# Hybrid block on one core: another order of the units of a head pair in the attention stage

## The reference, cut to what matters

```python
x = x + conv(gn(x))          # 8 images x 64 channels x 32x32; 9 bilinear samples of 4 corners each
t = to_tokens(x)             # 8 x 1024 tokens x 64
# attention: 16 heads of 64, causal, rotary, on layer-normed tokens
q, k, v = proj(ln_t(t));  q, k = rope(q), rope(k)
att = softmax(where(causal, q @ k.T / 8, -inf));  t = t + (att @ v) @ w_o.T
t = t + spectral(ln_t(t))
# inside conv: out = einsum('bkhwc,ock->bohw', sampled, w), where sampled is the
# weighted sum of 4 gathered corners for each of 9 taps
```

## Time and profile before

| | |
|---|---|
| median of 3 runs | 2944.49 us (2943.2 to 2948.28) |
| the profiled execution | 2945.84 us |
| its span | 2944.1 us |
| TensorE busy, mean granted clock | 2745.4 us (93%), 0.965 |
| VectorE, ScalarE, GpSimd busy | 2185.9, 1329.4, 1736.8 us |

### The profile page before, as it was taken

One profiled execution on the slowest core, in us unless ns is written; L12 is line 12 of the kernel. 1 busy time (PEld: TensorE's weight loads), 2 busy tenths in 40 slices (PEclk: granted clock), 3 DMA queues, 4 the chain that ended last, 5 costly groups with the idle time before them and its releaser, 6 DMA issues. The chain is left out here.

```text
span 2944.1 us, 60697 instructions
## 1 busy us (share of the span) xinstructions
PE 2745.4 (93%) x18761; PEld 1792.2 (61%) x18761; DVE 2185.9 (74%) x3909; ACT 1329.4 (45%) x1788; POOL 1736.8 (59%) x1832
## 2 busy tenths in 40 slices
PE   3638999999999999999999999999998799999998
PEld 1324565565655655655655655655655688888887
DVE  3446878888778788778788888888876675767676
ACT  1103444444444444444444444444443465656565
POOL 3745777777777777777777777777776670000000
PEclk8658999999999999999999999999999899999999
DMA  5541221222222222222222222243443553434343
GB/s 151 145 110 53 59 64 54 72 63 63 64 62 62 65 61 62 63 63 62 63 63 62 64 59 65 64 61 64 64 64 53 159 165 126 143 125 152 115 151 107
DMA packets 159644, 249.21 MB, mean 85 GB/s; under 512 B 71662, under 2 KB 93502, under 8 KB 159582
## 3 DMA queue, kind: packets, MB, share of 16 engines
q1 hardware_dynamic: 125902, 155.61, 18.6%
q0 software_dynamic: 33680, 92.71, 13.0%
HBM read 230.65 MB, written 17.04 MB: 84 GB/s over the span
## 5 line engine op out<-in xcount | busy, mean ns | idle before, releaser
L1085 ACT ACTIVATE attention_probs<-attention_pss 128x1024 f32<-128x1024 f32 x576 | 589.6, 1024 | 311.7 <-PE attention_pss L922 299.2
L1288 POOL DMA_INDIRECT attention_gat<-table,attention_idx x585 | 556.9, 952 | 200.2 <-issue 126.3
L922 PE MATMUL attention_pss<-attention_kq 64*128 64x512 f32 (+3 forms) x3072 | 651.9, 483 | 0.0
L1151 DVE TENSOR_REDUCE attention_mx_half<-attention_pss 128x2 f32<-128x1024 f32 (+3 forms) x520 | 513.2, 1020 | 98.4 <-PE attention_pss L922 98.4
L1024 PE MATMUL attention_psY<-attention_probs,attention_xt 128*64 128x512 f32 (+3 forms) x3120 | 574.2, 496 | 0.2 <-issue 0.2
L1644 DVE SCALAR_TENSOR_TENSOR spectral_eo<-spectral_psE,kept_sig,spectral_eo 64x512 fp32r<-64x512 f32 x512 | 384.0, 750 | 170.5 <-ACT spectral_eo L1619 164.4
L1245 POOL TENSOR_TENSOR attention_kq<-attention_tA,attention_tB 128x512 f32<-128x512 f32 x260 | 415.9, 1611 | 116.1 <-DVE attention_tB L1161 107.0
L1537 PE MATMUL spectral_psE<-spectral_tz,spectral_up 128*128 128x512 f32 (+1 forms) x2304 | 462.3, 358 | 6.0 <-DVE spectral_up L1635 5.8
L1619 ACT ACTIVATE spectral_eo<-spectral_psE,kept_sig 64x512 fp32r<-64x512 f32 x512 | 350.0, 684 | 244.4 <-PE spectral_psE L1537 239.4
L922 PE MATMUL attention_pss<-attention_rows_m,attention_ones 64*128 64x512 f32 (+2 forms) x1536 | 458.8, 530 | 0.0
L1537 PEld LDWEIGHTS spectral_psE<-spectral_tz,spectral_up 128*128 128x128 f32 x2304 | 386.7, 189 | 78.3 <-issue 6.3
(11 more groups left out here) (193 smaller groups left out, 3198.8 us busy)
## 6 DMA issues: line engine op xcount, KB each, us to landing
spectral_tz<-phis SPq DMA_DIRECT2D x128, 320.5 KB, 4.6
spectral_tz<-phis SPq DMA_DIRECT2D x128, 320.0 KB, 4.2
attention_xb<-xn SPq DMA_DIRECT2D x132, 256.0 KB, 3.8
attention_gat<-table,attention_idx POOLq DMA_INDIRECT x585
table<-front_pixT SPq DMA_DIRECT2D x32, 288.0 KB
attention_wt<-in_w SPq DMA_DIRECT2D x66, 128.0 KB, 3.6
attention_xt<-xt SPq DMA_DIRECT2D x18, 128.0 KB, 2.1
attention_xs<-in_x SPq DMA_DIRECT2D x65, 32.0 KB
```

Source lines behind the costliest of these rows:

```text
L922: ins = pe.matmul(out(n), left(rows), right(rows), **flags)
L1085: act.activation(probs[:, u[1], :, :].rearrange("p n q -> p (n q)"), pss[:, slot, :], ACT.Exp, scale=float(E) ** -0.5).then_inc(s_act, 1)
L1151: ins = dve.tensor_reduce(mx[:, :, i] if i < 4 else mx_half[:, :, i - 4, k0 // 4], scores, AX.X, ALU.max)
L1288: pool.indirect_dma_start(gat[:, n, :, :].rearrange("p q c -> p (q c)"), None, d.table.rearrange("r q c -> r (q c)"), bass.IndirectOffsetO ...
```

## The change

Three tables are replaced; no instruction is added or taken away in the loop, except that fold 1 leaves VectorE's stream and joins GpSimd's.

- Value units 0 to 4 now belong to the pair in hand (lag 0) and 5 to 8 to the pair before; before, 0 and 1 did and 2 to 8 lagged. Values 5 and 6 open the pair.
- The scores stand in longer runs: S 1 and 2, then 3 and 4, then 5 near the start; 6 and 7 and then 8 near the end. Before, 5 to 8 stood together in the last quarter.
- `("norm",)` stands behind the maxima k and a; `merge` and `row` are still near the end, and `("out", 1)` has moved from the middle to the place between `dX` and `row`.
- `("fold", 1)` has left `SEQUENCE` and follows fold 0 in `POOL_ORDER`; both now stand between `("add", 1)` and `("mask", 0)`, ahead of adds 2 and 3.
- `AHEAD` has its maxima in another order.

The new tables:

```diff
--- before.py
+++ after.py
@@ -652,20 +652,19 @@
     return max(K_AT[k0 // 4], Q_AT[i // 4])
 
 
-SEQUENCE = [("rope", 0), ("rope", 1), ("weigh", 0), ("upper", 0), ("rope", 2), ("upper", 1), ("value", 2, 1),
-            ("weigh", 1), ("value", 3, 1), ("value", 4, 1), ("S", 0), ("rope", 3), ("upper", 2), ("S", 1),
-            ("max", "a"), ("value", 5, 1), ("weigh", 2), ("value", 6, 1), ("max", "d"), ("max", "g"), ("upper", 3),
-            ("max", "h"), ("leave",), ("value", 7, 1), ("value", 8, 1), ("S", 2), ("fold", 1), ("S", 3),
-            ("max", "k"), ("out", 0), ("dT",), ("out", 1), ("max", "e"), ("S", 4), ("max", "i"),
-            ("value", 0, 0), ("max", "f"), ("max", "c"), ("dR",), ("norm",), ("S", 5), ("S", 6),
-            ("S", 7), ("max", "j"), ("S", 8), ("max", "b"), ("merge",), ("value", 1, 0), ("dX",),
-            ("row",)]
-POOL_ORDER = [("add", 0), ("add", 1), ("add", 2), ("mask", 0), ("add", 3), ("fold", 0), ("gather", 0),
-              ("gather", 1), ("mask", 2), ("token", 0), ("mask", 4), ("gather", 2), ("mask", 7), ("mask", 8),
-              ("token", 1)]
+SEQUENCE = [("value", 5, 1), ("value", 6, 1), ("weigh", 0), ("rope", 0), ("rope", 1), ("S", 0), ("rope", 2),
+            ("upper", 0), ("weigh", 1), ("S", 1), ("S", 2), ("weigh", 2), ("upper", 1), ("rope", 3),
+            ("S", 3), ("S", 4), ("leave",), ("max", "d"), ("value", 7, 1), ("value", 8, 1), ("S", 5),
+            ("max", "c"), ("upper", 2), ("upper", 3), ("out", 0), ("dT",), ("max", "f"), ("value", 0, 0),
+            ("max", "h"), ("max", "i"), ("dR",), ("max", "e"), ("max", "j"), ("S", 6), ("S", 7),
+            ("max", "k"), ("max", "a"), ("norm",), ("value", 1, 0), ("value", 2, 0), ("max", "b"), ("S", 8),
+            ("max", "g"), ("value", 3, 0), ("value", 4, 0), ("merge",), ("dX",), ("out", 1), ("row",)]
+POOL_ORDER = [("add", 0), ("add", 1), ("fold", 0), ("fold", 1), ("mask", 0), ("add", 2), ("add", 3),
+              ("gather", 0), ("token", 0), ("mask", 2), ("mask", 4), ("gather", 1), ("mask", 7), ("gather", 2),
+              ("token", 1), ("mask", 8)]
 AHEAD = [("rope", 0), ("rope", 1), ("upper", 0), ("upper", 1), ("rope", 2), ("rope", 3), ("upper", 2),
-         ("upper", 3), ("max", "a"), ("max", "d"), ("max", "c"), ("max", "b"), ("max", "g"), ("max", "h"),
-         ("max", "e"), ("max", "f"), ("max", "k"), ("max", "i"), ("max", "j"), ("merge",), ("row",)]
+         ("upper", 3), ("max", "d"), ("max", "c"), ("max", "a"), ("max", "b"), ("max", "f"), ("max", "h"),
+         ("max", "e"), ("max", "g"), ("max", "i"), ("max", "j"), ("max", "k"), ("merge",), ("row",)]
 
 
 BY_ACT = ("S", "row", "dT", "dR")
```

## The result

The changed kernel takes 2999.01 us (median of 4 runs, 2995.1 to 3000.96) against 2945.07 us (4 runs, 2943.2 to 2948.28). The ratio is 1.0179, with a 95% interval from 1.0166 to 1.0192: slower by 54 us. The prediction, 2971 us, had the sign and its range held the time, but the loss is twice what it forecast (+26 us). The profiled execution took 3000.94 us, its span 2999.2.

A forecast was written before the change was run, and what follows sets the result against it. TensorE, busy 594.73 of 600 us in mid-loop, was taken as the bound. Per pair -0.05 + 0.30 + 0.10 + 0.10 = +0.45 us, times 64, less 2.7: +26 us, so 2971 us predicted, range 2948 to 3000.

The forecast's parts named there:

- TensorE's own time: TensorE's time for the same 39 units reordered, one change of array form fewer: 0.05 us less a pair.
- chain of VectorE at the end of a pair: From k's end to `row`, VectorE needs 7.36 us against TensorE's 7.03 of work: `row` 0.30 us late a pair.
- S 1's slot: S 1 takes rope 1's slot and waits for VectorE's read: 0.1 us a pair (0 to 0.15).
- j's slot: Maximum j takes i's slot and waits for VectorE's read: 0.1 us a pair (0 to 0.25).
- The prediction's own sign of being wrong: The prediction is wrong if TensorE waits at `row` for nothing, or if its waits name POOL or the DMA.
- fold 1 where 1.4 was forecast: Fold 1 on GpSimd takes 1.4 us (1.3 to 2.63); GpSimd is no bound and the delay stays hidden by 0.3 us.
- Fold 1 of VectorE freed "where it is not needed": VectorE's 0.75 us for fold 1 is freed where it is not needed, so it gains nothing.
- The row's copy: The copy is there about 3.0 us after `row`'s end, S 0 starts 3.7 us after `row`: hidden by 0.7 us.
- The rival that it comes late: S 0 finds its row 1 us later than worked out: 0.4 us a pair, 2997 us; chance 0.04.
- The tail: Behind the last pair four value units remain instead of seven, which saves 2.7 us.
- that only the changes of form count: No wait comes out and fewer changes of array form make the pair 0.2 us shorter: 2930 us; chance 0.08.

The follow-up runs named there:

- experiment 2: Changed kernel with one Newton step instead of three in norm (6 of its 15 instructions left out): 2954.82 us, ratio 1.0027.
- experiment 1: Changed kernel with ScalarE's two waits at a score unit swapped, the wait for the scores now second: 2971.19 us, ratio 1.0086.
- experiment 5: Changed kernel with ScalarE's two waits at a score unit swapped and one Newton step instead of three in norm: 2931.82 us, ratio 0.9958.
- experiments 4 and 8: Kernel before with fold 1 alone moved to GpSimd: 2950.93 us; changed kernel with fold 1 back on VectorE ahead of maximum d: 2990.44 us.
- experiments 1 and 3: ScalarE's two waits at a score unit swapped, in the changed kernel (2971.19 us) and in the kernel before (2942.68 us).
- experiment 6: Changed kernel with maximum b moved ahead of norm and out 1 ahead of `dX`: 3011.27 us, ratio 1.0224.
- the fourth order: Another order, ScalarE's waits swapped: pair begins as in the kernel before, fold 1 on VectorE, norm between S 7 and j: 2898.18 us, ratio 0.9838.

## Why the prediction was wrong in size

The first table sets each term of the sum, in us a pair, against what the runs showed:

| term | forecast | bounds | measured |
|---|---|---|---|
| TensorE's own time | -0.05 | -0.2 to 0 | about -0.7 |
| chain of VectorE at the end of a pair, with the turn behind it | +0.30 | 0.1 to 0.45 | +0.72 |
| S 1's slot | +0.10 | 0 to 0.15 | +0.15 |
| j's slot | +0.10 | 0 to 0.25 | +0.24 |
| ScalarE at the score units: table load at a turn's S 0 | none | none | +0.33 |
| the same: the rest of what the swap gave | none | none | +0.16 |
| sum | +0.45 | | +0.82 |

(0.72 is experiment 2's 1.43 us a turn over two pairs, 0.33 and 0.16 are experiment 1's 0.66 and 0.31 over two. The first line is what is left: experiment 5's 31.07 less 31.39 is -0.32, and less the two slots -0.7. The slots' own lines are differences of unit distances; no run took them away. The terms add to 0.9; those that the runs removed together were worth 2.25 a turn and not 2.40.)

That the time fell into the range of 2948 to 3000, by 1 us, is luck: TensorE's own time came out 0.65 us a pair below its term, 42 us in all, and hid that much of what the waits cost beyond the forecast.

**Two steps failed.** The larger is the chain's wait, taken at `row` for 0.30 us a pair where it came out at `dX` and cost 0.72 with what follows; it has its own paragraph below. The other is not in the prediction at all: of ScalarE it costs nothing but the `upper` copies, and the runs showed 0.49 us a pair there, 0.33 of them the table load. The new table changes which activation comes first in the loop's body, and with it where the load runs. The load itself could be read in the trace of before: the view of instruction groups has it 32 times, at 1283 ns, with 3.9 us idle before it. In the changed kernel it is 168.1 us:

```profile
L1103 ACT ACT_TABLE_LOAD x32 | 41.1, 1283 | 3.9
```

```profile
L1084 ACT ACT_TABLE_LOAD x32 | 41.1, 1283 | 168.1 <-PE attention_pss L921 168.1
```

The Trainium skill gives the load's price ("ScalarE: Activation LUTs", What ACT_TABLE_LOAD costs): about 1283 ns, and for a switch to another set a drain of about 1380 ns with it. The first half agrees with every load here. The second doesn't show: the exponential starts 1.30 us after the load's start, and in experiment 1 the load starts 0.22 us after the activation ahead of it. Nor does it show at a real switch in the front stage of before, from the exponential (L612, to 9.05 us) to the square root (L614): the load runs from 9.07 to 10.35, and the root starts at 10.37. The page tells to save loads by grouping functions by set (Table sets: the hidden batching unit); here none was added, and the place alone cost 21 of the 54 us.

**The chain was right, its customer was wrong.** From k to `merge` 7.27 us were forecast and 7.25 measured, without rest. But the prediction compares it with TensorE's work at `row`, and the same chain has an earlier customer: `dX`, two units ahead, takes b's slot. It says so, and doesn't compare there. By its own prices b was read 0.04 + 1.14 + 0.34 + 3.76 + 0.60 = 5.88 us after k's end, and TensorE had 0.27 + 1.87 + 0.43 + 1.30 + 0.25 + 1.87 = 5.99 of work, a rest of 0.11. That is too little, since from b's read (1216.35) to `dX`'s start (1216.59) another 0.24 us pass; 0.05 had been taken for such a step. At j it does take 0.05, from i's read at 1206.88 to the weight load at 1206.93. But at `dX` the slot's wait stands ahead of a second wait, for norm's end: two instructions of the sequencer (L78 and L79, at 1216.39 and 1216.49) lie between b's read and the weight load at 1216.56. The wait that is met last stands first, as in ScalarE's code. The prediction's own sign of being wrong, that TensorE waits for nothing at `row`, came true: no wait is listed there, and its distance is 0.14 against 0.11 with the shorter chain. And a wait at `dX` costs more than its length. `dX` is longer by 0.30 to 0.47, `out` 1 behind it by 0.12 (1.02 against 0.90), `row` by 0.03, and the turn of the loop by 0.35 in every second pair. In the mean the first three make 0.54, already over the upper bound of 0.45, and the turn goes on top with 0.18 (experiment 2).

**TensorE's own time** fell by more than its bounds. In experiment 5 the turn costs nothing (value 5 takes 1.01 us in both pairs), where before it cost 0.47 us in the first; that is 0.24 a pair of the 0.7. The rest is spread over units that stand beside others than before. Added up over a second pair, and without the two slot waits, the maxima take 0.25 us less (e ends ahead of `dR`, behind which it stands), the value units 0.11, the scores and `row` 0.08 each. A bound drawn from one seam (0.15 us) was too narrow for that.

**The slot waits** were of the right kind: S 1's load starts 0.05 us after rope 1's read, and j's 0.05 us after i's. Both came out at their upper bounds.

**GpSimd** took 1.41 us for fold 1 where 1.4 was forecast. The first of the two groups is fold 0 (for the earlier trace rows):

```profile
L1274 POOL TENSOR_TENSOR attention_gat<-attention_gat 128x1152 f32<-128x1152 f32 x20 | 53.0, 2649 | 42.4 <-DVE attention_gat L1175 42.4
...
L1276 POOL TENSOR_TENSOR attention_smp<-attention_gat 128x576 f32<-128x576 f32 x20 | 28.1, 1407 | 3.6 <-POOL attention_gat L1274 3.6
```

No matmul waits for it, as said; that it costs nothing was wrong by 5 to 9 us (experiments 4 and 8), and no wait of TensorE names GpSimd for it. Fold 1 of VectorE freed "where it is not needed" stands: put back ahead of d, where VectorE was idle, it cost nothing. **The row's copy** landed 3.0 us after `row`'s end in the middle pairs, as worked out, and rope 1, the unit ahead of S 0, ended 3.8 to 4.1 us after it. The rival that it comes late held in the last ten pairs alone, once the orders were faster. **The tail** saved 1.7 us and not 2.7; 0.64 of the difference is the wait for a mask.

Of the rivals, that only the changes of form count looks like experiment 5, 2932 us against the 2930 named for it. But the nearness is chance: there the two slot waits are still in, 25 us, and TensorE's own time is down by 0.7 us a pair and not by 0.2. The Trainium skill's rule on draining at a change of mode had given the sign of TensorE's own time; the waits that outweighed it were outside its subject.

## What to carry to other kernels

Before you cost a new order, look on each engine for what comes first in the loop's body: a table load stands there, and it waits with whatever stands ahead of it as an instruction of its own. Compare a chain with the other engine's work at each of its customers, not only at the last. A small shortfall costs more than itself, since the engine that is never idle loses the lead of its sequencer, and with it what that lead had hidden. Put the wait that is met last on the instruction itself, and the one that has long been met ahead of it.

## What the runs showed of the hardware that I had not expected

- An ACT_TABLE_LOAD of 1.28 us came once in each turn of the loop. Behind a separate wait it starts when the wait is met; with only a wait that has long been met ahead of it, it started after 0.22 us of idling, right behind the activation ahead of it (experiment 1).
- A wait that an activation carries let it start 0.05 us after the scores' end; the same wait as an instruction of its own, 0.13 us (experiments 1 and 3).
- The turn of the loop on TensorE cost 0.47 us (before), 0.35 us (changed), 0.20 us (experiment 6) and nothing (experiments 2 and 5). The branch came 0.16, 0.19, 0.35 and over 1.1 us before `row`'s end, and the next matmul started 0.40, 0.28 and 0.13 us after that end, or with no gap. So what a turn costs depends on how far the sequencer is ahead when it reaches the branch.
- Indirect gathers of surplus tiles, all of whose indices are 0, took 2.6 times the DMA time of the others, with equal bytes, in experiment 5, and were as slow in the kernel before and the fourth order (32.3% and 36.0% of the DMA engines' time there, 12.3% to 13.0% in middle images). That the one row is the reason was not isolated.
